# Keys and values of the second cross attention from a context and weights split in two rounded parts

## The reference

```
qn = layernorm(x, ln_q_g, ln_q_b)
q = qn @ Wq * scale
kv = media @ Wkv
k, v = jnp.split(kv, 2, axis=-1)
sim = jnp.einsum('bhid,bhjd->bhij', q, k)
sim = jnp.where(media_mask[:, None, None, :], sim, neg_inf)
attn = jax.nn.softmax(sim, axis=-1)
out = jnp.einsum('bhij,bhjd->bhid', attn, v)
x = x + jnp.tanh(attn_gate) * (out @ Wo)
```

## Time and profile before

| | us |
|---|---|
| three runs, median (lowest, highest) | 4311.71 (4309.52, 4315.76) |
| the profiled execution, device time | 4311.72 |
| its span | 4310.1 |
| TensorE matmuls busy in the span | 3691.4 (86%) |
| VectorE, ScalarE, GpSimd busy | 2084.1, 1805.1, 1477.5 |
| from the first key chunk of cross1 to the end of its units | 2154.4 to about 3665 |

### The profile page before, as it was taken

One profiled execution on the slowest core, in us unless ns is written; L12 is line 12 of the kernel. 1 busy time (PEld: TensorE's weight loads), 2 busy tenths in 40 slices (PEclk: granted clock), 3 DMA queues, 4 the chain that ended last, 5 costly groups with the idle time before them and its releaser, 6 DMA issues. The chain is left out here.

```text
span 4310.1 us, 74835 instructions
## 1 busy us (share of the span) xinstructions
PE 3691.4 (86%) x24808; PEld 2343.4 (54%) x24808; DVE 2084.1 (48%) x3357; ACT 1805.1 (42%) x3374; POOL 1477.5 (34%) x1377
## 2 busy tenths in 40 slices
PE   5777766788888886897699999999999999688998
PEld 4544454333333334786455555555555556566886
DVE  3455523666666662452155555555555554102454
ACT  1222211566666663111145555555555555112343
POOL 0112101111111110000057767776777778001554
PEclk9899978999999999998799999999999999899999
DMA  2101022000000003322200000000000000422110
GB/s 95 64 31 41 21 83 73 9 19 17 19 19 19 18 9 106 118 87 74 96 23 14 29 27 14 27 14 27 14 29 26 14 13 11 140 74 112 52 36 11
DMA packets 85826, 185.89 MB, mean 43 GB/s; under 512 B 13152, under 2 KB 46304, under 8 KB 82784
## 3 DMA queue, kind: packets, MB, share of 16 engines
q1 hardware_dynamic: 83040, 172.95, 11.9%
q0 software_dynamic: 2432, 8.39, 0.5%
HBM read 119.16 MB, written 62.14 MB: 42 GB/s over the span
## 5 line engine op out<-in xcount | busy, mean ns | idle before, releaser
L1520 POOL TENSOR_TENSOR cross_acc<-cross_acc,cross_probs 128x512 f32<-128x512 f32 (+1 forms) x704 | 919.3, 1306 | 205.0 <-ACT cross_probs L1579 163.1
L1579 ACT ACTIVATE cross_probs<-cross_s,cross_bias 128x512 f32<-128x512 f32 (+1 forms) x832 | 530.1, 684 | 525.8 <-PE cross_s L1784 485.8
L1670 DVE TENSOR_REDUCE cross_partmax<-cross_r 128x1 f32<-128x400 f32 (+1 forms) x1024 | 540.6, 570 | 376.2 <-PE cross_r L1754 354.2
L1173 DVE TENSOR_REDUCE cross_partmax<-cross_m 128x2 f32<-128x800 f32 (+1 forms) x512 | 493.3, 990 | 299.4 <-PE cross_m L1264 297.8
L1085 ACT ACTIVATE cross_probs<-cross_s 128x512 f32<-128x512 f32 (+1 forms) x832 | 458.7, 596 | 169.2 <-PE cross_s L1284 164.1
L1797 PE MATMUL cross_av<-cross_probs,cross_v 128*64 128x256 f32 (+1 forms) x3328 | 458.0, 393 | 0.0
L1797 PEld LDWEIGHTS cross_av<-cross_probs,cross_v 128*64 128x64 f32 (+1 forms) x3328 | 199.2, 136 | 278.6 <-ACT cross_probs L1579 199.9
L1295 PE MATMUL cross_av<-cross_probs,cross_v 128*32 128x256 f32 (+1 forms) x3328 | 267.5, 393 | 58.3 <-ACT cross_probs L1085 58.3
L1264 PE MATMUL cross_m<-cross_ks,cross_qd 64*128 64x400 f32 (+1 forms) x1024 | 216.5, 442 | 78.3 <-DVE cross_ks L1161 37.0
L1033 POOL TENSOR_TENSOR cross_diag<-c_ident,cross_negmax 128x256 fp32r<-128x256 f32 x128 | 75.9, 615 | 588.3 <-DVE cross_negmax L1181 588.3
L1778 PE MATMUL cross_s<-cross_q_hi,cross_k_hi 64*128 64x256 f32 (+1 forms) x1664 | 253.8, 299 | 0.0
(11 more groups left out here) (256 smaller groups left out, 6486.3 us busy)
## 6 DMA issues: line engine op xcount, KB each, us to landing
cross_ct<-in_ctx_t SPq DMA_DIRECT2D x16, 801.0 KB, 4.9
d_cross<-cross_out SPq DMA_DIRECT2D x96, 128.0 KB, 1.8
d_cross<-query_pr SPq DMA_DIRECT2D x8, 1024.0 KB, 4.5
cross_qp<-d_cross SPq DMA_DIRECT2D x64, 128.0 KB, 2.2
out_at<-d_cross SPq DMA_DIRECT2D x8, 1024.0 KB, 5.3
mem_cn<-in_ctx_n SPq DMA_DIRECT2D x8, 832.0 KB, 6.4
ffn_ct<-in_ctx_t SPq DMA_DIRECT2D x8, 801.0 KB, 4.8
d_masked_ctx<-ffn_ctx_out SPq DMA_DIRECT2D x8, 801.0 KB, 7.5
```

The source lines that it names most:

```text
L1173: nc.vector.tensor_reduce(partmax[:, :, jt // 2, jt % 2, i:i + 1], m_pair(M_SET[q], w), AX.X, ALU.max).then_inc(maxed, 1)
L1520: nc.gpsimd.tensor_tensor(acc[0:w, g % 2], left, probs[0:w, slot % NPB], ALU.add).then_inc(added, 1)
L1579: nc.scalar.activation(probs[0:w, (g * KT + t) % NPB], src_, ACT.Exp, scale=XHD ** -0.5, bias=bias[0:w, p, t:t + 1]).then_inc(probs_ready, 1)
L1670: nc.vector.tensor_reduce(partmax[:, m, i:i + 1], r_ps[MAX_BANK[q]][:, 0:KCH[i][1]], AX.X, ALU.max).then_inc(maxed, 1)
```

## The change

`MaskedContext` now keeps, for a batch in which no key is valid, the context as it is and notes this in a flag per batch (`key_flag`, 0 there and 1 otherwise); query1 multiplies the normalised queries by the flag. So keys and values can both be made from the masked context. After L620 two new steps split it: ScalarE copies it rounded to float32r (`scalar_step`), GpSimd subtracts (`pool_step`); the store waits for GpSimd and carries both parts, 128 x 2 x 1602. ScalarE's copy of batch b stands behind the third Silu of batch b+1. In cross1 the weights are loaded as one tile and split by ScalarE and VectorE before the first unit; SyncE loads the two parts of the context in place of `ct` and `cm`; each float32 matmul of `k_chunk` and `v_tile` becomes three in float32r (high x high, high x rest, rest x high).

```diff
+        self.split = ph.sb("ctx_split", [P, 2, 2, NKP], F32R)
...
     def store(self, sp, u):
         b, p, _, _ = u
-        sp.wait_ge(self.ready, b + 1 + PRIME)
-        sp.dma_start(self.masked_d[b], self.out[:, p, :]).then_inc(self.stored[p], 16)
+        sp.wait_ge(self.lo_ready, b + 1 + PRIME)
+        sp.dma_start(self.masked_d[b], self.split[:, p].bitcast(F32)).then_inc(self.stored[p], 16)
+
+    def scalar_step(self, act, u):
+        b, p, _, _ = u
+        act.wait_ge(self.ready, b + 1 + PRIME)
+        act.wait_ge(self.stored[p], half(b, p) * 16 + PRIME)
+        self.nc.scalar.activation(self.split[:, p, 0], self.out[:, p], ACT.Copy).then_inc(self.hi_ready, 1)
+
+    def pool_step(self, pool, u):
+        b, p, _, _ = u
+        pool.wait_ge(self.hi_ready, b + 1 + PRIME)
+        self.nc.gpsimd.tensor_tensor(self.split[:, p, 1], self.out[:, p], self.split[:, p, 0], ALU.subtract
+                                     ).then_inc(self.lo_ready, 1)
...
         elif i == 2:
+            flag = self.c["key_flag"][:, b, :]
             ch.link(nc.vector.tensor_reduce(stat[:, 0:1], valid[:, 0:NK], AX.X, ALU.add))
+            ch.link(nc.vector.tensor_scalar(flag, stat[:, 0:1], 1.0, None, ALU.min))
+            ch.link(nc.vector.tensor_scalar(stat[:, 2:3], flag, -1.0, 1.0, ALU.mult, ALU.add))
         elif i == 3:
-            ch.link(nc.vector.tensor_tensor(kept[:], self.ct[:, p, :], valid[:], ALU.mult))
+            ch.link(nc.vector.scalar_tensor_tensor(kept[:], valid[:], stat[:, 2:3], self.ct[:, p, :], ALU.max, ALU.mult))
...
         else:
-            dve.wait_ge(self.stored[p], half(b, p) * 16 + PRIME)
+            dve.wait_ge(self.lo_ready, b - 1 + PRIME)
...
-                            last = nc.vector.tensor_scalar(xn[:, p, k], xs[:, k], b_norm[:, k:k + 1], None, ALU.add)
+                                last = nc.vector.tensor_scalar(xn[:, p, k], xs[:, k], b_norm[:, k:k + 1], scale_q[:, b, :],
+                                                               ALU.add, ALU.mult)
...
-                    sp.dma_start(ct[:, p], src["ctx_t"][b]).then_inc(loaded[p], 16)
-                    sp.dma_start(cm[:, p], masked_d[b]).then_inc(loaded[p], 16)
+                    sp.dma_start(c_hi[:, p].bitcast(F32), masked_d[b, :, 0]).then_inc(loaded[p], 16)
+                    sp.dma_start(c_lo[:, p].bitcast(F32), masked_d[b, :, 1]).then_inc(loaded[p], 16)
...
+                act.wait_ge(w_ready, 32)
+                for part in range(2):
+                    cols = slice(part * NP * P, (part + 1) * NP * P)
+                    nc.scalar.activation(w_hi[:, cols], w[:, cols], ACT.Copy).then_inc(w_hi_ready, 1)
...
+                for part in range(2):
+                    cols = slice(part * NP * P, (part + 1) * NP * P)
+                    dve.wait_ge(w_hi_ready, part + 1)
+                    nc.vector.tensor_tensor(w_lo[:, cols], w[:, cols], w_hi[:, cols], ALU.subtract).then_inc(w_lo_ready, 1)
...
-                    nc.tensor.matmul(r_ps[K_BANK[i]][:, 0:w], wk[:, g], cm[:, p, k0:k0 + w], start=True, stop=True
-                                     ).then_inc(kp_ready, 1)
+                    nc.tensor.matmul(o, w_hi[:, cols], c_hi[:, p, keys], start=True, stop=False)
+                    nc.tensor.matmul(o, w_hi[:, cols], c_lo[:, p, keys], start=False, stop=False)
+                    nc.tensor.matmul(o, w_lo[:, cols], c_hi[:, p, keys], start=False, stop=True).then_inc(kp_ready, 1)
...
-                    nc.tensor.matmul(r_ps[bank][0:w, :], ct[:, p, t * P:t * P + w], wv[:, h], start=True, stop=True
-                                     ).then_inc(vp_ready, 1)
+                    nc.tensor.matmul(o, c_hi[:, p, keys], w_hi[:, cols], start=True, stop=False)
+                    nc.tensor.matmul(o, c_hi[:, p, keys], w_lo[:, cols], start=False, stop=False)
+                    nc.tensor.matmul(o, c_lo[:, p, keys], w_hi[:, cols], start=False, stop=True).then_inc(vp_ready, 1)
...
                             nc.scalar.activation(act_g[:, m % 2], in_ps[m % 4][:, 0:S], ACT.Silu).then_inc(act_ready, 1)
+                            if masked and m == 2 and before:
+                                masked.scalar_step(act, before)
```

## The result

The changed kernel takes 4253.46 us (median of 4 runs, 4243.05 to 4256.31), the kernel before 4310.61 (4 runs, 4305.13 to 4315.76). The ratio is 0.9863, 95% interval 0.9842 to 0.9884: faster by 1.4%, where 1.8% was forecast (4235 us). The profiled execution took 4243.05 us (span 4241.2), the lowest of its four; a second profile of the same kernel, taken with the experiments, has 4252.72.

What follows compares the result with a forecast made beforehand. TensorE was taken to bound cross1. Value tiles -41, key chunks -38 and 3 back make -76 us, with 0.6 more for the first chunks at half clock: 4311.7 - 76.6 = 4235 us; 8 in 10 for 4225 to 4255.

Steps and rivals of the forecast that it cites:

- (a): cross1, slot 2: VectorE and ScalarE, not TensorE, set the time to key chunk 1; 19 us lost; chance 0.09.
- (b): ffn0 becomes bound by VectorE, slowed by GpSimd, say 2 us in each of 8 batches: 16 us back; chance 0.06.
- TensorE is the limit in cross1: In a 200 us stretch inside cross1 TensorE's matmuls are busy for 199.56 us, so its work sets the time.
- Value tiles 41 us, key chunks 38: cross1: three float32r passes for four save 0.196 us on 208 value tiles, 0.15 us on 256 key chunks.
- The third weight load is hidden: cross1: weight loads inside a block of three float32r matmuls overlap running matmuls and add no time.
- (c): cross1: two more weight loads exposed per block, 0.1 us each; 23 us slower, 4335; chance 0.03.
- 3 us back at the tie: cross1, slot 2: VectorE's rest part delays the next reduction, losing 0.05 us per unit, 64 units.
- The start of cross1 costs nothing: Splitting the weights on ScalarE and VectorE ends before the first key chunk's context arrives; cost 0, uncovered 4 us once.
- ffn0 costs nothing: ffn0: ScalarE's copy and GpSimd's subtraction delay VectorE by 2 us, within TensorE's slack; bad end 0.4 us per batch.
- Last store hidden, query1 0: ffn0's doubled last store takes 7.6 us, done before the last output store; query1's flag multiply 0 to 2 us, taken 0.

Runs made afterwards that it cites:

- e5: Changed kernel with the values' product ahead of the key chunk and value tile in slots 1 to 3: 4276.53 us, ratio 0.9913 to the kernel before.

## Why the prediction was right, and where it was off

The forecast, faster with 1.8% against 1.4% measured, lay in the right mechanism, and the result in the range (4225 to 4255) at its upper end. The range holds it only because it was widened to take in rivals (a) and (b), and (a)'s mechanism did not happen; the forecast's own range, from the ends of its two terms, was 4225 to 4243 and missed. By its own steps:

- *TensorE is the limit in cross1.* Right: 67 us came, and another 89 by taking away a third of the passes.
- *Value tiles 41 us, key chunks 38.* The mis-sized terms. The step that failed is "a pass costs its columns plus between 0.003 and 0.013 us ... I take 0.006 to 0.007". The earlier trace rows had 0.18 us for 400 columns and 0.11 to 0.12 for 256, both about 8% over; I read the excess as a fixed amount and split it over the pair. By the column it makes 0.231 us for 512, outside my bounds. In cross1 the values alone gave 32.5 us (below the low end of 37), the keys alone 30.8 (below 33).
- *The third weight load is hidden.* Right, 0.18 us between records. Rival (c) and the rule behind it (the Trainium skill, "TensorE: Matmul & The Clock Gate", Part 3) are refuted for these shapes: all three use all rows, and no load shows. But its side, slower, is where four products came out, by the pace of the columns.
- *3 us back at the tie.* Not seen; 0.11 of 0.12 us arrives. Rival (a) is wrong for the change; e5 shows that it names a real chain.
- *The start of cross1 costs nothing.* Right: the first chunk still waits for its context, at 2150.45 with 15.65 us idle before it against 16.12.
- *ffn0 costs nothing.* Wrong by 4 to 5 us: nine profiles with the subtraction on GpSimd have 2.2 to 7.0 us more than before's 271.3, on average 4.3; the changed kernel's own two have 5.2. The step: "Two operations of 1 us could each double: 2 us later ... just in time". The estimates of the operations were right (ScalarE's copy 1.53 us for 1.7, GpSimd's subtraction 3.0 to 4.4 for 4.1 at most), the effect on VectorE was not: one operation is held for all that is left of GpSimd's, some 3 us. The slack was smaller too: with L617 3.4 us late TensorE waited 1.7, so it covered 1.7 us where I had reckoned with 2. This is rival (b) at a quarter to a third of its price, since only one to four batches pay.
- *Last store hidden, query1 0.* Right: the store goes out at 1979.28, takes 5.5 us instead of 7.6, and the last output store follows at 1989.24; query1's length is within 1.3 us of before's in all profiles.

What the forecast has no term for is out1, which the change does not touch: 114.4 and 115.2 us before, 115.5 to 118.1 in eleven profiles of changed kernels, 117.0 on average. It goes with the granted clock: 0.87 or 0.88 in the seven profiles of 114.4 to 116.8 us, 0.85 or 0.86 in the six of 117.8 to 118.1; what lowers the clock was not tried. The changed kernel's own two profiles add up, against the two before, to -67.1 in cross1, +5.2 in ffn0, -0.6 in query1 and +0.9 in out1, -61.6 us; the ratio of the second set of runs, 0.9861 of 4315.47, makes -60.0.

## What to carry to other kernels

Splitting a float32 matmul into three float32r products saves less than the quarter that counting passes promises, 18 to 19% at full clock here, and the fourth product would make it a loss; where the only row of a pass has another length, compare two lengths before you call an excess fixed. Before giving a spare GpSimd an operation on SBUF, look at what VectorE does at that time: its own 1.82 us were cheaper than 3.6 us of a helper that stopped it. An order that looks as if it waits can be hiding a chain, so price what the moved block was covering, and over several units.

## What was not expected of the hardware

- A float32r pass goes at 0.443 ns a column at a granted clock of 1.00 (0.231 us for 512, 0.118 for 256, 0.004 of each by the instruction), a float32 pass at 0.417 (0.214 for 512); at a granted clock of 0.50 float32r takes 0.833 ns a column (0.333 for 400), with nothing over. So it loses 6% to something that does not scale with TensorE's clock or hides at half of it; which, no run here tells.
- VectorE's one-operand passes over 128x1602 (0.98 us) took 2.9 to 4.4 us when they met GpSimd's two-operand subtraction, which is the rest of GpSimd's instruction plus their own time.
